# Two-layer token mixer with expert routing: attention in two passes, the routing inside the second, code one-hots on ScalarE

## The reference, cut to what matters

```python
# layer 0: a recurrence of 16 states, h = tanh(h @ A.T + u_t), then out = (h @ Wo.T + bo) * gate ...
# layer 1, attention over the 4 sequences at one position (axis of length 4), 16 heads of 16:
scores = einsum('ibhd,jbhd->ijbh', q, k) / 4;  causal; softmax with +1 in the denominator
out = einsum('ijbh,jbhd->ibhd', attn, v)
# layer 1, mixture of 8 experts, two per token, capacity 2048 rows each:
topv, topi = top_k(softmax(xt @ wg), 2)
pos = running count of each expert's tokens
disp[topi, pos] = xt ;  y = relu(disp @ w1 + b1) @ w2 + b2 ;  out = sum(gate * y[topi, pos])
x = x + s * silu(g)
```

## Time and profile before

| what | us |
|---|---|
| median of 3 runs (1437.73 to 1439.36) | 1438.14 |
| the profiled execution's own time | 1429.75 |
| its span in the profile | 1427.9 |
| PE busy / DVE / ACT / POOL in it | 1175.3 / 1016.6 / 628.1 / 625.2 |
| mix, from 14.5 to about 269.8 | 255 |
| attend, from 269.8 to 574.7 | 305 |
| route, from 575.3 to 630.9 | 56 |
| experts and combine, from 631.5 | 796 |

### The profile page before, as it was taken

How to read it: one execution, slowest core, us unless ns; L and a number is a source line. 1 busy time by engine, 2 the same in 40 slices (tenths; PEclk the granted TensorE clock), 3 DMA queues, 4 the chain that set the end, 5 groups by cost and what they waited for, 6 DMA issues and landing times. The chain is left out here.

```text
span 1427.9 us, 22572 instructions
## 1 busy us (share of the span) xinstructions
PE 1175.3 (82%) x7547; PEld 802.9 (56%) x7547; DVE 1016.6 (71%) x1931; ACT 628.1 (44%) x960; POOL 625.2 (44%) x530
## 2 busy tenths in 40 slices
PE   4899999588888884146999989999899998999910
PEld 3566666366666663134566666666666665666610
DVE  7757667759888887885767667676576765776638
ACT  4855555233333441003544545445455454553522
POOL 5500000028777777013454544645546455464430
PEclk9999999799999997557999999999999999999965
DMA  8260000001111110105555445554555545555569
GB/s 328 83 214 1 1 1 1 15 30 31 31 31 31 32 31 16 59 19 109 105 109 104 76 99 101 112 106 71 108 92 113 109 66 114 89 111 104 66 168 347
DMA packets 148960, 122.55 MB, mean 86 GB/s; under 512 B 88400, under 2 KB 133328, under 8 KB 148720
## 3 DMA queue, kind: packets, MB, share of 16 engines
q1 hardware_dynamic: 114912, 83.90, 20.1%
q0 software_dynamic: 25200, 35.85, 16.4%
q10 hardware_dynamic: 8736, 1.33, 0.5%
HBM read 58.91 MB, written 44.30 MB: 72 GB/s over the span
## 5 line engine op out<-in xcount | busy, mean ns | idle before, releaser
L1722 ACT ACTIVATE e_h_all<-e_pH,e_b1c,e_h_scale 128x512 f32<-128x512 f32 x256 | 199.6, 780 | 283.9 <-PE e_pH L1763 256.1
L1777 PE MATMUL e_pY<-e_w_hi,e_h_hi 128*128 128x256 f16 x1024 | 279.6, 273 | 17.1 <-DVE e_w_lo L1597 10.0
L1506 POOL DMA_INDIRECT e_xg<-xn_rows,e_icol x140 | 162.4, 1160 | 287.1 <-DVE e_icol L1538 254.3
L1778 PE MATMUL e_pY<-e_w_lo,e_h_hi 128*128 128x256 f16 x1024 | 279.1, 273 | 0.0
L1779 PE MATMUL e_pY<-e_w_hi,e_h_lo 128*128 128x256 f16 x1024 | 279.1, 273 | 0.0
L1521 POOL DMA_INDIRECT expert_sums<-e_yo,e_dcol x128 | 213.0, 1664 | 76.7 <-issue 43.0
L1640 DVE TENSOR_TENSOR e_h_lo<-e_h_all,e_h_hi 128x512 f16<-128x512 f32 x256 | 177.3, 693 | 66.3 <-ACT e_h_hi L1722 56.6
L1761 PE MATMUL e_pH<-e_xT,e_w_hi 128*128 128x512 f16 x512 | 195.1, 381 | 26.5 <-DMA e_xT<-e_xs 17.6
L1762 PE MATMUL e_pH<-e_xT,e_w_hi 128*128 128x512 f16 x512 | 194.9, 381 | 0.0
L1763 PE MATMUL e_pH<-e_xT,e_w_lo 128*128 128x512 f16 x512 | 194.8, 380 | 0.0
L1777 PEld LDWEIGHTS e_pY<-e_w_hi,e_h_hi 128*128 128x128 f16 x1024 | 100.1, 98 | 42.9 <-DVE e_h_lo L1640 24.6
(11 more groups left out here) (251 smaller groups left out, 2169.0 us busy)
## 6 DMA issues: line engine op xcount, KB each, us to landing
raw<-expert_w SPq DMA_DIRECT2D x18, 1024.0 KB
expert_sums<-a_zero SPq DMA_DIRECT2D x10, 1024.0 KB, 10.7
x_st<-x SPq DMA_DIRECT2D x16, 512.0 KB, 9.1
xn_rows<-c_xn SPq DMA_DIRECT2D x16, 512.0 KB, 3.0
f_ya<-expert_sums SPq DMA_DIRECT2D x16, 512.0 KB, 7.3
out<-x_st SPq DMA_DIRECT2D x8, 1024.0 KB, 8.5
e_xg<-xn_rows,e_icol POOLq DMA_INDIRECT x140
e_xT<-e_xs SPq DMA_TRANSPOSE x136
```

The costliest lines, as they stand in the source:

```text
L1506: pool.indirect_dma_start(xg[:, q, 0:D + E], None, v.xn3_dram, bass.IndirectOffsetOnAxis(icol[u][:, q:q + 1], axis=0), bounds_check=N - 1, ...
L1722: last = act.activation(dst, pH[h % NPH][:, :], ACT.Relu, bias=b1c[eu][:, h:h + 1], scale=h_scale[eu][:, 0:1])
L1777: pe.matmul(pY[:, q, :], h_hi[:, h, cols], w2_hi[:, h, :], start=(h == 0), stop=False)
L1778: pe.matmul(pY[:, q, :], h_hi[:, h, cols], w2_lo[:, h, :], start=False, stop=False)
```

## The change

- **mix.** PE's product with the identity is gone. DVE adds `u_st` to the product in PSUM and writes `r_in`; ACT takes the tanh of that. So each of the 48 steps now passes PE, DVE and ACT. DVE has it at four places: after the gate's sum, after `finish`, after `normalise` and after `units`.
- **attend** is split into two passes over the tiles. The first has `layer0`, `scale`, `normalise`, `turn` and the logits of all tiles; the transposed rows stay in `prod_st`. The second has q, k, v, softmax and values. q, k and v have PSUM buffers of their own (c_pY, c_pX, c_pT). The first of the four products of values is made by DVE, the other three and the sums by POOL. The bias constants are made by POOL in the first pass.
- **route** is no block any more. DVE makes the choices in tiles 0 and 1 of the second pass, the count in tile 2, the places in tile 4, the low one-hots of two groups in each of tiles 5 to 12, the table in tile 14. ACT makes the code one-hots as relu(code - code*(iota - high)^2): 8 squares and 8 relus of 128 columns for a group, two groups in each of tiles 5 to 12. PE sums the groups of tile t-2 after v of tile t.
- The first expert's weights are loaded when the table is done. Some buffers share memory.

The core of the diff (lines that only rename or rearrange memory are left out):

```diff
                 def step(t, slot):                          # mix, DVE, new
+                    for j, n, l in steps_at(t, slot):
+                        if j:
+                            if j >= 2:
+                                dve.wait_ge(state, j - 1)
+                            ...
+                            dve.wait_ge(carried, j)
+                            dve.tensor_tensor(rin[j % 2][:, first:NCH], pR[j % 2][:, first:NCH], v.u_st[:, l, first:NCH],
+                                              ALU.add).then_inc(summed, 1)
@@ mix, PE
-                        ins = pe.matmul(pR[j % 2], ident, v.u_st[:, l, :], start=True, stop=(j == 0),
-                                        skip_group_check=True)
-                        if l:
-                            ins = pe.matmul(pR[j % 2], v.at_blk, v.h_st[:, l - 1, :], start=False, stop=True,
-                                            skip_group_check=True)
+                            if l:
+                                ins = pe.matmul(pR[j % 2], v.at_blk, v.h_st[:, l - 1, :], start=True, stop=True)
@@ attend, DVE, second pass
+                products(0)
+                scores(0)
+                for t in range(NT):
+                    if t + 1 < NT:
+                        products(t + 1)
+                    if t < TOPK:
+                        ...
+                        choose(t)
+                    elif t == 2:
+                        along()
+                    elif t == 4:
+                        places()
+                    for n in hots_of(t):
+                        one_hots(n)
+                    if t == HOTS_AT + K2 // NB // HOTS + 1:
+                        tables()
+                    weights(t)
+                    if t + 1 < NT:
+                        scores(t + 1)
@@ in weights(t)
+                    part, row = value_parts(t, 0)
+                    dve.tensor_tensor(v.prod_st[:, t, :].rearrange("p (i h d) -> p i h d", i=B, h=H), part, row,
+                                      ALU.mult).then_inc(o_ready, 1)
@@ attend, ACT, second pass
+                def code_hots(n):
+                    m = n % 2
+                    act.wait_ge(placed, 1)
+                    ...
+                    for i in range(NB):
+                        h = NB * n + i
+                        last = act.activation(apart[:, i, :], v.iota, ACT.Square, bias=less_hi[:, h:h + 1])
+                    last.then_inc(squared, 1)
+                    act.wait_ge(squared, n + 1)
+                    for i in range(NB):
+                        h = NB * n + i
+                        last = act.activation(ohc[m][:, i // INNER_N, :, i % INNER_N], apart[:, i, :], ACT.Relu,
+                                              scale=less_code[:, h:h + 1], bias=code[:, h:h + 1])
+                    last.then_inc(ohc_ready, 1)
+                take_qk(0)
+                take_v(0)
+                take_qk(1)
+                for t in range(NT):
+                    act.wait_ge(ex_in, t + 1)
+                    act.activation(ex[:, :, :, :], ex[:, :, :, :], ACT.Exp).then_inc(ex_out, 1)
+                    if t + 1 < NT:
+                        take_v(t + 1)
+                    if t + 2 < NT:
+                        take_qk(t + 2)
+                    for n in hots_of(t):
+                        code_hots(n)
@@ attend, PE, second pass: q, k and v of tile t as before, then
+                    for h in hots_of(t - 2):
+                        pe.wait_ge(ohl_ready, h + 1)
+                        pe.wait_ge(ohc_ready, h + 1)
+                        for a in range(WIDE):
+                            for i in range(INNER_N):
+                                last = pe.matmul(ptab, ohl[h % 2][:, a, :, i], ohc[h % 2][:, a, :, i],
+                                                 start=False, stop=False, skip_group_check=True)
+                        last.then_inc(used[h % 2], 1)
```

More of the change, by code:

```diff
@@ L208, in program @@
         attend(nc, v)
+        experts(nc, v)
         front.close()
[L210 to L218, removed]
         combine(nc, v)
@@ L405, in mix @@
         pR = [pT[:, n, 0:NCH] for n in range(2)]
+        rin = [sb(f"r_in{n}", [P, NCH]) for n in range(2)]
+        carried = sem("r_carried")
         passed = sem("a_passed")
@@ new lines, in _, with products @@
+                linked(dve.memset(sc[:, :, :, :], -1e30))
+                for t in range(NT):
+                    layer0(t)
+                def products(t):
+                    dve.wait_ge(q_evac, t + 1)
+                    dve.wait_ge(k_evac, t + 1)
+                    for j in range(B):
+                        w = B - j
+                        last = dve.tensor_tensor(qk[:, PAIR0[j]:PAIR0[j] + w, :], q[:, j:B, :],
+                                                 spread(k[:, j, :], w), ALU.mult)
+                    last.then_inc(qk_ready, 1)
@@ new lines, in _, with columns, one_hots @@
+                counted = iota[:, :, :].unsqueeze(1).broadcast_to([P, WIDE, P, INNER_N])
+                def columns(ap, n):
+                    cols = ap[:, n * NB:(n + 1) * NB].rearrange("p (a u) -> p a u", u=INNER_N)
+                    return cols.unsqueeze(2).broadcast_to([P, WIDE, P, INNER_N])
+                def one_hots(n):
+                    m = n % 2
+                    if n >= 2:
+                        dve.wait_ge(used[m], n // 2)
+                    dve.tensor_tensor(ohl[m], counted, columns(lo, n), ALU.is_equal).then_inc(ohl_ready, 1)
@@ new lines, in turn_logits @@
+                def turn_logits(t):
+                    pe.wait_ge(l_taken, t + 1)
+                    pe.transpose(pL[t % 2][:, P:2 * P], lgT[t % 2][:, :], ident).then_inc(l_turned, 1)
+                output(0)
+                output(1)
+                for t in range(NT + 2):
+                    if t + 2 < NT:
+                        output(t + 2)
+                    if t < NT:
+                        turn(t)
+                    if 0 <= t - 1 < NT:
+                        logits(t - 1)
+                    if 0 <= t - 2:
+                        turn_logits(t - 2)
```

830 lines of the change are left out of this document (400 added, 430 removed).

## The result

| | before | changed |
|---|---|---|
| median, 4 runs each on one chip | 1437.93 us (1436.15 to 1439.36) | 1475.30 us (1473.68 to 1478.90) |
| ratio, with its 95% interval | | 1.0276 (1.0257 to 1.0295) |
| profiled execution: time, span | 1429.75, 1427.9 us | 1473.68, 1471.6 us |
| attend's first matmul | 269.8 | 263.1 |
| from there to `experts`' first instruction on VectorE | 361.7 us (to 631.48) | 411.6 us (to 674.65) |

The change makes the kernel 2.8% slower. By the last three rows mix gave 6.7 us, the two passes with the routing took 49.8 us more, and the rest 0.5: 43.7 us in all, as in the spans. The medians are 37.4 us apart, because the profiled execution of the kernel before was 8.2 us faster than its median and that of the changed kernel only 1.6.

The account below looks back on a forecast made before the run. Stages follow each other; in attend PE was busy 203 and DVE 208 of 236 us. Attend with route +46.8 and mix -5 gave +41.8; from 1438.1 the forecast was 1480 us, range 1453 to 1497.

Parts of the forecast that it names:

- mix: Block mix, sum with u moved to DVE: -0.4 us in each of 12 tiles, -5 in all, bounds -10.5 and +5.
- the ring: Second pass, tiles 5 to 12: ScalarE's groups and TensorE's sums, q and k wait in a circle; 23.4 us a round, 187.2 in eight.
- The stall that I charged with 0.5 us: In mix, step 1's sum on DVE stands behind `finish`, so 0.5 us of each tile's saving comes back.
- The upper bound that I gave for mix, +5: In mix, a second stall of the same size as the first would make the block's term +5 us.
- First pass: Attend's first pass: `layer0` 4.72 us a tile with one more wait, 3 for POOL; second pass starts 88.6 after attend's start.
- Tiles 0 to 4: Second pass: plain tile 12.0 us, five tiles with routing work 78.3, evacuation of k of tile 7 starts at 195.4.
- more contention: Rival, 12%: DVE's new product of values and `layer0` lose time beside POOL; 12 us more, 1492.
- the clock holds: Rival, 22%: PE stays at 2.4 GHz in tiles 5 to 12; rounds of 21.1 us, eight of them 18 less, 1462.
- faster: Rival, 7%: ACT's one-hots cost 0.17 us each, a round 15.5, time 1417; turning point 0.26 each.
- The end: Second pass, from the last evacuation of k through products, table, softmax and POOL's remaining operations: 25.3 us, to 407.9.
- The signs named in advance: k's evacuations 21 to 24 us apart, ACT not idle, clock 0.6 to 0.9, `layer0` every 4.7 to 5.2, mix tile 12.4 to 12.6.

Follow-up runs that it names:

- e5: The changed kernel with 6 and 11 unread filler matmuls ahead of TensorE's waits for the first and second group of a tile; 1.0164 of the kernel before.
- e2: The changed kernel with the code one-hots made on VectorE instead of ScalarE, TensorE's order as changed; 0.9942 of the kernel before.
- e1: The changed kernel with TensorE's sums of tile t-3 between k and v of tile t, instead of tile t-2's behind v; 0.9865 of the kernel before.
- e10: The changed kernel with TensorE's sums of tile t-3 between k and v, and the first product of values on GpSimd again; 0.9925 of the kernel before.
- e8: The changed kernel without GpSimd's six value operations of a tile; one execution, no ratio, attend with routing 390.5 us, rounds 23.83 us.

## Why the prediction was right

The forecast was 1480 us, 2.9% above before; measured is 1475.3, 2.8% above. As a difference in the profiled execution it was +41.8 and became +43.9; between the medians it is +37.4. The mechanism was the forecast one, the ring that TensorE's queue closes, and its round was 0.2 us off. That the sum came out only 2 us off is partly luck: attend with route was 3.0 us longer than forecast (410.9 in place of 407.9), mix 1.7 us shorter.

- **mix**, forecast -5: it was -6.7. The tile went from 12.89 to 12.31, not to 12.5. The stall that I charged with 0.5 us costs 0.3. These are the changed kernel's DVE sum of step 1 and what PE does then:

```profile
135.46 0.28 DVE L570 TENSOR_TENSOR r_in<-a_pT,u_st 128x128 f32<-128x128 f32 x1
```

```profile
134.30 1.88 PE L713 MATMUL a_pS<-prod_st,first 128*128 128x512 f32 x4
136.23 0.49 PE L721 MATMUL a_pT<-shared,late 128*128 128x128 f32 x2
```

  `finish` does hold the sum back (PE had step 1's product at 134.5). The tanh is done at 136.18, just as L713 ends, so the profile shows no idle time of PE; but the next product starts 1.93 us after L713, where in the kernel before the product behind the same four matmuls (there L693) started after 1.72 (137.40 to 139.12), and the matmul behind it comes another 0.1 late. Of the four times 0.22 us, 0.58 remain. The upper bound that I gave for mix, +5, was wrong by its own terms: a second stall of 0.5 us in 12 tiles makes about +1.
- **First pass**: second pass forecast 88.6 us after attend's start, measured 89.0 (q's first matmul at 352.07). That is luck, errors that cancel: `layer0` takes 4.37 us, not 4.72 (278.40 to 282.77), and the 3 us for POOL beside it are not there, but after the first `layer0` DVE waits another 7.1 us for PE's output in this pass, and from its last instruction to q it is 9.7 us, not 8.
- **Tiles 0 to 4**: evacuation of k of tile 7 forecast 195.4 us after attend's start, measured 196.8. The first `products(1)` came earlier (109.7, not 112.0), since the clock was back before q started. The plain tile was 12.75 us, not 12.0: the value product cost 1.23, less than the 1.5 I allowed, but products and difference cost 5.05 and 1.15 beside GpSimd. The five tiles were also summed 0.8 us too low: the choices, the count and the places are 19.1 us in the earlier trace rows, and 18.3 stand in the tiles. The rival "more contention" was right that VectorE loses more time beside GpSimd, but put it in the wrong place: the value product and `layer0`, where it looked for it, lost nothing (1.23 and 4.37 us), while the products of q and k and the difference did. Its 12 us were too dear, because DVE does not bound in the rounds.
- **The ring**: forecast 23.4 us a round and 187.2 in all, measured 23.60 and 188.8. The parts: a group 5.91 from start to start (forecast 5.7), PE's waits 3.04 and 4.83 (2.7 and 5), the clock, by e5, 1.75 to 2.1 (2.3). At full clock a round is 21.74, not 21.1: two groups 0.4 more, and PE's last eight matmuls 0.92, not 0.65. The case "the clock holds" is refuted by the granted 0.79. The case "faster" is refuted by the prices: 16 squares and 16 relus take 11.8 us, 0.37 each, over its 0.26.
- **The end**: forecast 25.3 from the evacuation of k, measured 25.3 (648.66 to 673.99). `experts` and combine: +0.5.
- **The signs named in advance**: the evacuations of k (22.7 to 23.9 us apart), PE's waits for the relus, ACT without idle time through both groups and the clock of 0.79 came as said. Two did not: `layer0` comes every 4.37 us, not 4.7 to 5.2, and a tile of mix takes 12.31, not 12.4 to 12.6.

## What to carry to other kernels

When work moves onto an idle engine, follow one item through all queues until it comes back to where it started, and add up that circle, before adding up the engine's busy time. ScalarE had room for 14.6 us in a tile of 16.9, but TensorE's sums stood ahead of the matmuls that ScalarE waited for, and the tile became 23.6. The remedy is then the order of a queue, here one place later, rather than faster instructions: the change together with that order beats the kernel before by 1.3 to 1.7%, while the version with the same work on the engine that does it five times faster (e2) is 0.6% faster than before, since that engine was already the fuller one.

## What the runs showed that I had not expected

GpSimd and VectorE wait for each other, instruction by instruction. These are VectorE's first product of values and GpSimd beside it, in e1:

```profile
503.26 1.23 DVE L1121 TENSOR_TENSOR prod_st<-c_att,c_v 128x1024 f32<-128x1024 f32 x1
```

```profile
503.36 2.48 POOL L1037 TENSOR_TENSOR c_pv<-c_att,c_v 128x768 f32<-128x768 f32 x1 [4.51 <-DVE c_att L1115]
```

In e10, where VectorE sums scores at that time, the same GpSimd operation takes 1.50 us; here it takes 0.98 more, and VectorE's product still had 1.13 to go when it started. VectorE's sums of scores (tensor_reduce) take 2.99 us in e1, with GpSimd at work, and in e8 without it: these two do not disturb each other. The Trainium skill ("SBUF — State Buffer", section "SBUF: two separate sides") says that a VectorE instruction with two SBUF inputs and a GpSimd one that reads SBUF lock each other out for their whole length; e1, e8 and e10 agree, by the 0.98 us here, and by products of 3.02 us alone, 5.07 beside GpSimd in e1 and 5.91 in e10. I had used that rule as a small rival. It settles more: where a 0.42 us difference waits out a 1.8 us sum of GpSimd, the cost of moving an operation between the two depends on which instructions then meet, as e10 showed against my expectation.
